# Four fused attentions: another order for the side pieces of the 32-step loop

## The reference

```
x = x + L0_attn(layernorm(x))   # 16 heads of 16, 8 key heads, rope, window of 64 + 64 global, ALiBi
x = x + L0_ffn(layernorm(x))
x = x + L1_attn(layernorm(x))   # causal, 16 heads
x = x + L1_ffn(layernorm(x))
x = x + L2_attn(layernorm(x))   # causal, rope
x = x + L2_ffn(layernorm(x))
x = x + L3_attn(layernorm(x))   # not causal, heads and batches regrouped before the output product, bias
x = x + L3_ffn(layernorm(x))
```

## Time and profile before

| | us |
|---|---|
| median of three executions | 1944.53 |
| lowest, highest | 1933.18, 1951.77 |
| the profiled execution, its own time | 1942.08 |
| its span in the trace | 1940.3 |
| the four loops of 128 steps together | 1042.14 |

### The profile page before, as it was taken

The page is one execution under the profiler, slowest core; times in us unless marked ns, Lnnn a source line. Parts: engine busy times, 40 slices in busy tenths (PEclk is TensorE's granted clock), DMA queues, the critical chain, the costliest instruction groups (busy, mean ns, idle before and its releaser), DMA issues. The chain is left out here.

```text
span 1940.3 us, 28833 instructions
## 1 busy us (share of the span) xinstructions
PE 1628.8 (84%) x10648; PEld 942.5 (49%) x10654; DVE 1179.9 (61%) x2595; ACT 865.3 (45%) x1360; POOL 477.8 (25%) x594
## 2 busy tenths in 40 slices
PE   4989999899999999911499999869998999998676
PEld 2334443478855556501245555546775344433433
DVE  2677777343255665469857676456454777775476
ACT  1255555433215555522025445437673366566322
POOL 4222210023213312030222330016664422210100
PEclk9789999999999999965699999969999999999798
DMA  7351350100064335010245424031113355140322
GB/s 244 81 130 52 85 135 2 66 1 0 1 182 126 94 87 153 2 50 0 70 124 152 123 64 120 1 123 50 50 50 93 110 126 150 36 120 1 118 88 88
DMA packets 68688, 162.29 MB, mean 84 GB/s; under 512 B 10013, under 2 KB 15526, under 8 KB 67562
## 3 DMA queue, kind: packets, MB, share of 16 engines
q1 hardware_dynamic: 68554, 160.52, 29.2%
HBM read 111.06 MB, written 53.09 MB: 85 GB/s over the span
## 5 line engine op out<-in xcount | busy, mean ns | idle before, releaser
L1079 DVE TENSOR_REDUCE a_mx<-PS 128x1 f32<-128x512 f32 (+3 forms) x768 | 395.0, 553 | 184.3 <-PE PS L1321 113.0
L1262 ACT ACTIVATE a_pT<-PS 128x1024 f32<-128x1024 f32 (+3 forms) x384 | 308.6, 811 | 222.4 <-PE PS L1345 154.5
L1316 PE MATMUL PS<-a_k,a_q 64*128 64x512 f32 (+3 forms) x768 | 228.6, 413 | 30.4 <-DVE a_mx L1079 24.5
L405 DVE CUSTOM_DVE_ANT_0 PS<-PS,a_dist 128x448 f32<-128x448 f32 x256 | 156.2, 642 | 59.6 <-PE PS L650 58.3
L1336 PE MATMUL PS<-a_q,a_k 64*128 64x512 f32 (+3 forms) x768 | 174.2, 433 | 6.2 <-issue 3.2
L1359 PE MATMUL PS<-a_pT,a_va 128*32 128x512 f32 (+3 forms) x1536 | 166.8, 506 | 5.7 <-ACT a_raw L1220 5.7
L122 PE MATMUL PS<-cst 128*128 128x512 f32 x248 | 131.1, 657 | 44.5 <-PEq L66 35.2
L555 ACT ACTIVATE a_pT<-PS 128x448 f32<-128x448 f32 (+1 forms) x256 | 123.5, 542 | 95.4 <-PE PS L673 95.0
L1316 PEld LDWEIGHTS PS<-a_k,a_q 64*128 64x128 f32 x768 | 105.7, 186 | 102.6 <-DVE a_mx L1079 87.8
L1336 PEld LDWEIGHTS PS<-a_q,a_k 64*128 64x128 f32 x768 | 77.2, 185 | 107.2 <-issue 78.5
L2046 POOL TENSOR_TENSOR f_h_low<-f_prod,f_h_high 128x512 fp32r<-128x512 f32 x84 | 110.2, 1318 | 60.2 <-ACT f_h_high L2233 57.8
(11 more groups left out here) (355 smaller groups left out, 3449.9 us busy)
## 6 DMA issues: line engine op xcount, KB each, us to landing
spread_scratch<-a_high SPq DMA_DIRECT2D x96, 256.0 KB, 7.3
a_q<-spread_scratch SPq DMA_DIRECT2D x96, 256.0 KB, 5.7
a_k<-spread_scratch SPq DMA_DIRECT2D x96, 256.0 KB, 6.4
f_gb<-gate_rows SPq DMA_DIRECT2D x68, 256.0 KB, 5.2
spread_scratch<-a_low SPq DMA_DIRECT2D x48, 256.0 KB, 7.8
a_q<-window_scratch SPq DMA_DIRECT2D x32, 256.0 KB, 5.4
a_k<-window_scratch SPq DMA_DIRECT2D x32, 256.0 KB, 6.3
window_scratch<-a_high SPq DMA_DIRECT2D x24, 256.0 KB, 3.5
```

What stands on the lines that cost most here:

```text
L405: dve.tensor_tensor_reduce(PS[:, 4 + a, 0:KW], PS[:, 4 + a, 0:KW], dt_[:, off:off + KW], 1.0, 3e38, ALU.add, ALU.min, mx[:, gg % 2, qt, 2 ...
L1079: dve.tensor_reduce(mx[:, gg % 2, qt, 2 * half + a:2 * half + a + 1], PS[:, 4 + a, 0:kw], AX.X, ALU.max).then_inc(max_done, 1)
L1262: act.activation(pT[:, N // 2 % 2, N % 2, :, q0:S], PS[:, 2 * (N % 2):2 * (N % 2) + 2, q0:S], ACT.Exp, scale=SCALE).then_inc(exp_done, 1)
L1316: mm = pe.matmul(ps[:, 0:kw], q[rows, b % 2, pair, qt * P:(qt + 1) * P], k[rows, b % 2, pair, 0:kw], start=True, stop=not causal)
```

## The change

Only the dictionaries `plan`, `swaps` and `raised` of both functions change, that is, in which step each piece, exchange and split is done. No instruction is added or removed, and no size changes. Projections, outputs, groups and maxima come to even steps; turns, heads and the second of two neighbouring pieces go to odd ones (in attention 1 and 2 one group stays at step 3, and in attention 3 the outputs are at odd steps). The steps at which VectorE and GpSimd do the layer norm of a later batch stay.

```
 attention_window:
-        plan = {1: ("turn", 1, 0), 2: ("turn", 1, 1), 3: ("group", -1, 3), 4: ("project", 1, 0), 5: ("values", 1, 0),
-                6: ("minima", 0, 1), 8: ("turn", 1, 2), 9: ("turn", 1, 3), 10: ("project", 1, 1), 11: ("group", 0, 0),
-                13: ("project", 1, 2), 14: ("minima", 0, 2), 16: ("heads", -1, 1), 17: ("outputs", -1, 0),
-                18: ("outputs", -1, 1), 19: ("group", 0, 1), 21: ("heads", 0, 0), 22: ("minima", 0, 3),
-                27: ("group", 0, 2), 30: ("minima", 1, 0)}
-        swaps = {5: 0, 11: 1, 14: 2}
-        raised = {7: 0, 12: 1, 15: 2}
+        plan = {0: ("turn", 1, 0), 1: ("turn", 1, 1), 2: ("project", 1, 0), 3: ("values", 1, 0), 4: ("group", -1, 3),
+                5: ("turn", 1, 2), 6: ("minima", 0, 1), 7: ("turn", 1, 3), 8: ("project", 1, 1), 9: ("heads", -1, 1),
+                10: ("project", 1, 2), 12: ("group", 0, 0), 14: ("minima", 0, 2), 16: ("outputs", -1, 0),
+                18: ("outputs", -1, 1), 20: ("group", 0, 1), 22: ("minima", 0, 3), 24: ("heads", 0, 0),
+                28: ("group", 0, 2), 30: ("minima", 1, 0)}
+        swaps = {3: 0, 9: 1, 11: 2}
+        raised = {5: 0, 11: 1, 13: 2}
 attention_quads:
         if scrambled:
-            plan = {0: ("outputs", -1, 5), 1: ("turn", 1, 0), 2: ("turn", 1, 1), 3: ("group", -1, 3), 5: ("heads", -1, 3),
-                    6: ("maxima", 0, 1), 7: ("outputs", -1, 6), 8: ("outputs", -1, 7), 9: ("project", 1, 0),
-                    10: ("project", 1, 1), 11: ("group", 0, 0), 12: ("project", 1, 2), 13: ("heads", 0, 0),
-                    14: ("maxima", 0, 2), 15: ("outputs", 0, 0), 16: ("outputs", 0, 1), 17: ("project", 1, 3),
-                    18: ("values", 1, 0), 19: ("group", 0, 1), 20: ("values", 1, 1), 21: ("heads", 0, 1),
-                    22: ("maxima", 0, 3), 23: ("outputs", 0, 2), 24: ("outputs", 0, 3), 27: ("group", 0, 2),
+            plan = {0: ("outputs", -1, 5), 1: ("turn", 1, 0), 2: ("turn", 1, 1), 4: ("group", -1, 3), 6: ("maxima", 0, 1),
+                    7: ("heads", -1, 3), 8: ("project", 1, 0), 9: ("outputs", -1, 6), 10: ("project", 1, 1),
+                    11: ("outputs", -1, 7), 12: ("group", 0, 0), 14: ("maxima", 0, 2), 15: ("heads", 0, 0),
+                    16: ("project", 1, 2), 17: ("outputs", 0, 0), 18: ("project", 1, 3), 19: ("outputs", 0, 1),
+                    20: ("group", 0, 1), 22: ("maxima", 0, 3), 23: ("heads", 0, 1), 24: ("values", 1, 0),
+                    25: ("outputs", 0, 2), 26: ("values", 1, 1), 27: ("outputs", 0, 3), 28: ("group", 0, 2),
                     29: ("heads", 0, 2), 30: ("maxima", 1, 0), 31: ("outputs", 0, 4)}
         else:
-            plan = {1: ("turn", 1, 0), 2: ("turn", 1, 1), 3: ("group", -1, 3), 6: ("maxima", 0, 1), 11: ("group", 0, 0),
-                    14: ("maxima", 0, 2), 16: ("heads", -1, 1), 17: ("outputs", -1, 0), 18: ("outputs", -1, 1),
-                    19: ("group", 0, 1), 21: ("heads", 0, 0), 22: ("maxima", 0, 3), 23: ("values", 1, 0),
-                    24: ("values", 1, 1), 27: ("group", 0, 2), 30: ("maxima", 1, 0)}
-            for i, n in enumerate((4, 7, 9, 12) if rope is not None else (8, 9, 10, 12)):
-                plan[n] = ("project", 1, i)
-        swaps = {5: 0, 8: 1, 10: 2, 13: 3} if rope is not None else {}
-        raised = {6: 0, 9: 1, 11: 2, 14: 3} if rope is not None else {}
+            plan = {0: ("turn", 1, 0), 1: ("turn", 1, 1), 3: ("group", -1, 3), 4: ("project", 1, 0), 6: ("maxima", 0, 1),
+                    8: ("project", 1, 1), 9: ("heads", -1, 1), 10: ("project", 1, 2), 12: ("group", 0, 0),
+                    14: ("maxima", 0, 2), 16: ("project", 1, 3), 18: ("outputs", -1, 0), 20: ("group", 0, 1),
+                    22: ("maxima", 0, 3), 24: ("outputs", -1, 1), 25: ("values", 1, 0), 26: ("values", 1, 1),
+                    28: ("group", 0, 2), 29: ("heads", 0, 0), 30: ("maxima", 1, 0)}
+        swaps = {5: 0, 9: 1, 11: 2, 17: 3} if rope is not None else {}
+        raised = {7: 0, 11: 1, 13: 2, 19: 3} if rope is not None else {}
```

## The result

| | before | after |
|---|---|---|
| median | 1940.97 us (4 runs) | 1892.72 us (4 runs) |
| lowest, highest | 1933.18, 1951.77 | 1888.34, 1894.97 |
| profiled execution, its span | 1942.08, 1940.3 | 1893.01, 1891.2 |

The ratio is 0.9753, 95% interval 0.9724 to 0.9781. The forecast of 1911 us had the sign right; the range of 1894 to 1941 missed the time by 1.3 us. The gain in the profiled executions is 49.1 us where 33.8 were worked out.

What follows compares the result with a forecast made beforehand. TensorE was taken as bound by waits for VectorE's reductions at odd steps. Attentions 9.1, -0.6, 3.0 and 1.8 us plus groups 20.5 made 33.8 us: 1942.1 to 1908.3 profiled, 1911 us as median, range 1894 to 1941.

Steps and rivals of the forecast that it cites:

- The bound: Four loops: TensorE's score tiles at odd steps wait for VectorE's reductions; 87.8 us of waits in attentions 1 to 3.
- a falling busy time: Four loops: TensorE's busy time would fall with their length, since it had contained waiting; no size given.
- The walk through the earlier trace: Attention 1: with a group's transposes gone from the odd step, reductions start 0.74 us earlier; even-step price near 0.
- The groups: All attentions: 54 groups go from odd steps (0.47 us each) to even (0.05 to 0.15), gaining 20.5 us.
- Other pieces: All moves but the groups: 9.1 us in attention 0, -0.6 in 1, 3.0 in 2, 1.8 in 3.
- projection 2 at 10 in attention 0: Attention 0: the pair of steps holding the moved projection 2 would take under 5 us.
- attention 2's pair 4, 5: Attention 2, steps 4 and 5: 1.60 us of waiting for GpSimd's split goes, from 5.64 to near 4.1 us.
- no wait on a fetch at step 20: Attentions with rotations: the last fetch for head group 0 still lands in time for step 20; no stall.
- The clock: TensorE's granted clock taken as 1.00 (2.4 GHz) in the windows; a change would make the sum wrong.
- Rival 2: Loops: more is hidden than counted, groups free and outputs at attention 3's odd steps no dearer; 1900 us, chance 0.10.
- Rival 1: Loops: gaps stay and only change place, division delaying reductions; 1942 us, chance 0.20 together with rival 4.
- Rival 4: Step 20: a transfer comes late, each us beyond slack costing 6 us; chance 0.20 together with rival 1.

Runs made afterwards that it cites:

- e15: Changed kernel, in attention 1 alone projection 3 at step 12, outputs 1 at 20, groups 0 and 1 at 16 and 24; 1891.60 us, ratio 0.9752.
- e11: Kernel before, only the 54 groups moved to even steps and what stood there one step earlier; 1942.99 us, ratio 1.0021.
- e8: Changed kernel, in attentions 1 and 2 projection 3 at 17 and outputs 0 at 19 instead of 16 and 18; 1899.43 us, ratio 0.9779.
- e9: Kernel before, two idle matmuls added at the end of step 25 in attention 0, 26 in attention 3, batches 0 and 1; 1943.78 us, ratio 1.0028.

## Why the prediction missed

**The bound: right.** TensorE waits at odd steps for the reductions, and pieces at even steps fill that time: the waits fell from 87.8 to 60.7 us, the idle of the loops by 39.2. That its busy time contains waiting rests on the pairs of the earlier trace rows. The sign the prediction named for it, a falling busy time, came (11.4 us fewer) but proves nothing, since 43.5 us less at half clock shorten the busy time too. The walk through the earlier trace rows is of the steps 12 to 16 of that batch, not 3 to 8 as the rows' heading says; it is the same place in the eight, so the reading stands.

**The groups: the mechanism right, the size wrong.** The term was 54 x (0.47 less 0.05 to 0.15) = 20.5 us; the runs show 46 x 0.58 less 8 x 0.15, 25.4. Two errors in it work against each other. The 0.47 was measured against a false twin, the pair after (3.74 us), which is 0.11 us longer than the bare 3.63 at its own place. In attention 1 such a pair, 12 and 13, is 3.63 us with no group in it or before it (e15), so that length belongs to the place in the eight. The figure of attention 0 was then carried to the other three, where the earlier trace rows have no bare twin for it either. And all 54 were taken to be covered, though the last batch has no score tiles from step 20 on; there a group costs 0.73 at the even step. Elsewhere the price near 0, argued from the walk through the earlier trace rows, holds to 0.02 us.

**Other pieces: over-sized, 13.3 for 8.6 us.** One price for an even step was carried to all. The projection costs 0.42 at the fifth step of an eight, 0.97 at the first and 0.61 at the third in attention 3 (4.84 and 4.14 at 8 and 10, over 3.87 and 3.53), 0.97 where 0.57 was taken. Two moves of attention 3 have no term in the sum: projection 2 leaves 12 for 16 and loses some 0.4 us a batch, values 0 leave 18 for 24 and lose 0.5. Outputs 1 at 24 with values at 25 makes 6.10 us in attention 1, so that attention lost 1.6 and not 0.6 us there. Three single claims held: projection 2 at 10 in attention 0 under 5 us (4.51), attention 2's pair 4, 5 near 4.1 (4.06), no wait on a fetch at step 20. Attention 1 did gain least, 6.4 us (4 predicted), attention 0 most, 22.1 (some 14).

**The clock: the step that failed.** The prediction took TensorE at 2.4 GHz throughout, from the 1.00 in its windows, and put the rest under "what would make it wrong". The windows are clean pairs; the profile's clock line and the 0.95 of attention 0's whole loop were there to be read. By the table some 16.5 us of the gain in the first pair of traces, 10.1 with the second of after, came from fewer half-clock stretches. That the rest fits, 34.0 us for 33.8, is luck: the two mis-sized terms cancel (+4.9 and -4.7). So without the clock the forecast of 1911 would have been right; with it the time fell just under the range.

**The rivals.** Rival 2's 1900 us came nearest, and its premise of free groups was right for 46 of 54; its other one, outputs free at odd steps of attention 3, was not: the pair 16, 17 of batch 3 took 4.60 us with outputs 0 at 17, and 3.58 before with outputs 1 at 16. Rival 1, that the gaps only change place, is excluded for the changed order, but e11 shows what it warned of: with the groups alone every us is taken back, by displaced projections and by a piece queued behind GpSimd's work. Rival 4's late fetch did not come. The Trainium skill's rule in "Perfetto Trace Analysis", section Optimization Strategy, that a repeating gap can mean too little PSUM, is a possibility there; the consequence that the prediction drew, that the order gives nothing, did not bear out: with the same two score banks the order alone took 50.6 us from the loops, some 34 of them without the clock. On the clock, the Trainium skill's "TensorE: Matmul & The Clock Gate", section HAM oscillation — how this bites in real kernels, says that waits between groups of matmuls can send TensorE back to half rate. Its case is a loop that waits for DMA longer than it multiplies. The trace agrees in kind, with 0.50 in the pair behind the waits at 211.85, 1.71 of 5.49 us, in a loop otherwise 93% busy; the seven stretches without a wait are not of that kind.

**Open.** Why the same wait in attention 0 is followed by half clock in some executions and not in others, and why seven stretches in attention 3 follow no wait; no run here tells. That the changed kernel's remaining time at half clock could be removed by taking the layer norm out of the steps 24 and 25 was not tried.

## What to carry to other kernels

Price a moved piece against a bare stretch at the same place of the cycle: in a steady schedule the same piece cost 0.58 us at one step and 0.00 at the next, and a twin from the neighbouring place in the cycle hid a fifth of that. Move the whole set or nothing, since the place that a piece needs is held by another: groups alone gave 0, all together 48 us. Treat the end of the pipeline by itself: where the work ahead has run out, nothing is hidden (0.73 us for 0.00). And before an estimate lay the clock record over the stretches in question; a wait of 1.4 us cost 2.2 us more in the half-rate pair behind it.

## What was not expected of the hardware

- TensorE's granted clock falls to 0.50 inside a loop in which TensorE is 93% busy, in stretches of 3.4 to 17 us. Most follow idle time of some 1 to 2 us, but seven, in attention 3, follow less than 0.4 us (e8: 7.67 of 7.92 us busy). In one kernel all ten places were the same in two executions, in the other they were not.
- At half clock the same matmuls do not take twice as long in the step: a pair of 4.22 us became 6.43 (that its waits shrink meanwhile is argued: 3.69 of 4.21 us are busy in e9, 6.31 of 6.43 at 217.34).
- Idle matmuls in the wait kept the clock up in two of four places and cost what they saved (6.67 us for 6.76; 10.31 us for 5.49 where they ran at 0.67).
